# First cross attention: the rows of the context laid out by partition, 24 KB in one run instead of twelve runs of 2 KB

## The chip, the core and the metric

One core of one Trainium2 chip. The time is that of one execution on the device, in microseconds; of the kernel before there are three runs, and the number compared is their median.

## What is computed

A two-layer Perceiver block on x (8 batches of 64 rows of 512) and a context `ctx_1024` (8 batches of 1601 rows of 512), all float32. Every layer is a cross attention, an attention and an FFN, each added to x. The change lies in the very first of them:

```python
ex = jnp.einsum('bld,ed->ble', ix, W) + b          # ix = layernorm(x)
eother = jnp.einsum('bld,ed->ble', iother, W) + b  # iother = the context
scores = jnp.einsum('bld,bmd->blm', ex, eother)
attn = jax.nn.softmax(scores, axis=-1)
aligned = jnp.einsum('blm,bmd->bld', attn, iother)
```

The rest (a WKV recurrence, a product-key FFN, a 16-head cross attention on the same context, a sliding-window attention and a quantized linear layer) is as before.

## The kernel before, in words

The program is written by hand for each engine: every engine has its own list of instructions, and semaphores order them. All loads are issued by SyncE (SP), in the order in which its list has them, onto one DMA queue. Each waits only for the semaphore that tells that its buffer is free. A load raises its own semaphore by 16 when it has landed.

The first cross attention works on pairs of batches, p = 0 to 3 (a pair is 2 x 64 rows of x, so all 128 partitions). With g = W(Wx + b), computed on TensorE by the helper `product` (L416, matmuls at L420), the scores of a pair are g times the context, and the output is the softmax times the context. So the context is needed in two layouts:

- **Columns** (`load_columns`, L586 to 589, from `in_ctx_t`): the context transposed, the contraction over partitions. A pair has four pieces c = 0 to 3 of 4, 4, 2 and 3 tiles of 128 keys (`PIECE_TILE`, L63); each piece is two loads (one for each batch of the pair) into the slots of piece c. The host has already laid this array out by partition, so a partition's part of a piece is one run: 512 keys x 4 x 4 B = 8 KB for pieces 0 and 1, 4 KB for piece 2, 5 KB for piece 3. Piece c of pair p waits until the scores of piece c of pair p - 1 are done (`s1`, L602 to 604).
- **Rows** (`load_rows`, L580 to 584, from `in_ctx`): the context as it is, keys on the partitions, 12 full tiles of 128 rows in one load of 3072 KB (L583) and the last 65 rows in one of 130 KB (L584), for each of the two batches. Partition p of tile t is row 128 t + p, so a partition takes twelve runs of 2 KB, 256 KB apart. There are two sets of buffers (`cn`, L371); pair p >= 2 waits for the outputs of pair p - 2 (`pv1`, L606).

SP's order is: x, the two forms of W and the vectors (L575 to 578), columns (0, piece 0), (0, piece 1), rows(0); after the first layernorm columns (0, 2) and rows(1); after the g products (L598, L599) columns (0, 3); then for p = 1, 2, 3 the four pieces of columns(p), and for p = 2 and 3 rows(p) behind them (L601 to 607). Behind all that come the weights of the next layer (L609, L610), and after the last output those of the FFN (L613 to 617; `in_f` at L617 is read in runs of 4 KB with 16 KB from one partition's run to the next, `in_f` at L620 in runs of 2 KB).

TensorE goes through the pairs in the order `ORDER1` (L52 to 60): s(0), s(1), pt(0), o(0), s(2), pt(1), o(1), s(3), pt(2), o(2), pt(3), o(3). Here s is `scores1` (L957 to 971, matmuls at L968; piece c waits for its columns at L962), pt is `probabilities1` (transposes of the exponentials, L979), and o is `outputs1` (L982 to 994, 52 matmuls at L992, 13 tiles by two batches; it waits for the rows at L985). s(p) goes into the score banks of `SC` or `SB` by p's parity. Between s and pt, VectorE takes the maximum (`maximum1`, L1319) and ScalarE the exponential; after pt both copy the transposed probabilities out (L916, L918), and after o VectorE adds the output to X (L1337), which also frees the banks for s(p + 2) (L959, L960).

Of the kernel before, what the change touches and what calls it, by code (L numbers as in the profile page):

```python
# [12 lines left out]
P = 128  # L13
B, T, D = 8, 64, 512
NC = D // P
NT = B * T // P
M = 1601
MF = M // P
MR = M - MF * P
# [55 lines left out]
def piece_n(c, pad=0):  # L75

    k = piece_keys(c)
    return k.stop - k.start + pad * ((k.stop - k.start) % 2)
# [210 lines left out]
MID = 4  # L289


def build(nc, x, ctx_, W0, vecs, Wk, Wv, Wr, Wo, ctrl, f1, f2, Wq4, Wk4, Wv4,
          Wp4, bp4, Wq5, Wk5, Wv5, Wo5, wq, ws, bq, W0t, ctxt, tie, out):
    x = x.rearrange("b t d -> (b t) d").rearrange("(tt p) d -> p tt d", p=P)
    out = out.rearrange("b t d -> (b t) d").rearrange("(tt p) d -> p tt d", p=P)
# [4 lines left out]
    with ExitStack() as es:  # L300
# [8 lines left out]
        def sem(name):  # L309
            if name not in sems:  # L310
                sems[name] = es.enter_context(nc.semaphore(name))
            return sems[name]
# [75 lines left out]
        def inc(ins, name, by=1):  # L388
            return ins.then_inc(sem(name), by)
# [183 lines left out]
        def _(sp):  # L573
# [6 lines left out]
            def load_rows(p):  # L580
                for w in range(2):
                    dst, b, name = cn[p % 2][w], 2 * p + w, f"cn{p % 2}{w}_in"
                    inc(sp.dma_start(dst[:, 0:MF, :], ctx_[b, 0:MF * P, :].rearrange("(t p) d -> p t d", p=P)), name, 16)  # L583
                    inc(sp.dma_start(dst[0:MR, MF, :], ctx_[b, MF * P:M, :]), name, 16)  # L584

            def load_columns(p, c):  # L586
                n, at = NC * piece_n(c, 1), NC * piece_keys(c).start
# [3 lines left out]
            load_columns(0, 0)  # L591
            load_columns(0, 1)
            load_rows(0)
            for tt in range(NT):
                sp.wait_ge(*filled("ln0", tt))
            load_columns(0, 2)
            load_rows(1)
            sp.wait_ge(*filled("g", 3))  # L598
            sp.wait_ge(*filled("exb", 0))  # L599
            load_columns(0, 3)  # L600
            for p in range(1, NT):  # L601
                for c in range(KC):  # L602
                    sp.wait_ge(sem("s1"), KC * (p - 1) + c + 1)
                    load_columns(p, c)
                if p >= 2:
                    sp.wait_ge(sem("pv1"), p - 1)  # L606
                    load_rows(p)
# [1136 lines left out]
def laid_out(inputs):  # L1744


    import numpy as np

    ctx = inputs["ctx_1024"]
    padded = np.concatenate([ctx, np.zeros((B, M % 2, D), ctx.dtype)], axis=1)  # L1750
    pieces = [padded[:, PIECE_TILE[c] * P:][:, :piece_n(c, 1)] for c in range(KC)]

    ctx_t = np.concatenate([c.reshape(B, -1, NC, P).transpose(0, 3, 2, 1).reshape(B, P, -1) for c in pieces], axis=2)

    def by_head(w):

        return w.T.reshape(2, 4, 2, HD, D).transpose(0, 2, 1, 3, 4).reshape(D, D)

    laid = {
        "x": inputs["x"], "ctx": ctx, "W0": inputs["L0_xattn_W"],  # L1760
        "vectors": np.concatenate([inputs[n].reshape(-1, P).T for n in _VECTORS], axis=1),
        "Wk": inputs["L0_attn_Wk"].T, "Wv": inputs["L0_attn_Wv"].T, "Wr": inputs["L0_attn_Wr"].T,
        "Wo": inputs["L0_attn_Wo"].T,
        "controller": inputs["L0_ffn_controller"], "f1": inputs["L0_ffn_f1"], "f2": inputs["L0_ffn_f2"],
        "Wq4": inputs["L1_xattn_Wq"].T, "Wk4": inputs["L1_xattn_Wk"].T, "Wv4": inputs["L1_xattn_Wv"].T,
        "Wp4": inputs["L1_xattn_Wp"].T, "bp4": inputs["L1_xattn_bp"],
        "Wq5": inputs["L1_attn_Wq"].T, "Wk5": inputs["L1_attn_Wk"].T, "Wv5": inputs["L1_attn_Wv"].T,
        "Wo5": by_head(inputs["L1_attn_Wo"]),

        "wq": np.ascontiguousarray(inputs["L1_ffn_weight_q"].T).view(np.int32),  # L1770
        "ws": inputs["L1_ffn_weight_scale"], "bq": inputs["L1_ffn_bias"],
        "W0t": inputs["L0_xattn_W"].T, "ctx_t": ctx_t,

        "tie": np.repeat(np.linspace(0.0, 1e-6, NE, dtype=np.float32), ES)[:, None],
    }
    return {name: np.ascontiguousarray(a) for name, a in laid.items()}
# [16 lines left out]
```

## Time and profile before

| | us |
|---|---|
| median of 3 runs (lowest, highest) | 1229.19 (1227.73, 1231.67) |
| the profiled execution's own time | 1230.53 |
| its span | 1228.8 |
| lies outside the span (1230.53 - 1228.8) | 1.7 |

The profile and all its views are of that one execution. Its times count from the start of the span. TensorE is busy for 93% of the span, the 16 DMA engines for about a quarter of it, nearly all of that in the first sixth. A granted clock of 1.00 is TensorE's full speed of 2.4 GHz and 0.50 is 1.2 GHz. The DMA share of a stretch is summed over packets that overlap, so it can be a little over 1.

### The profile page before, as it was taken

The page shows a single profiled execution, that of the slowest core. Times are in us where ns is not written, and L with a number is a line of the kernel's source. Part 1 is how long each engine was busy: PE and PEld are TensorE (multiplying, and loading weights), DVE is VectorE, ACT ScalarE, POOL GpSimd, SP SyncE. Part 2 cuts the span into 40 slices and gives each one's busy share as a digit, 9 for nine tenths or more (in the row PEclk, how much of TensorE's full clock was granted, in tenths as well). Part 3 has the DMA queues.
Part 4 walks back from the last instruction along what each step waited for, and adds up shares of the span by engine and source line. Part 5 has one row for each costly group of instructions (what it writes and reads, how often), then busy time and mean ns, then how long its engine had stood idle before and what let it go on. Part 6 is the DMA issues. An engine that isn't in the chain of part 4 may idle for free.

```text
span 1228.8 us, 34222 instructions
## 1 busy us (share of the span) xinstructions
PE 1148.2 (93%) x15680; PEld 853.1 (69%) x15680; DVE 619.9 (50%) x978; ACT 433.2 (35%) x824; POOL 320.0 (26%) x362
## 2 busy tenths in 40 slices
PE   6879979878799999999999999999999999999996
PEld 3434434368488788788788888788878878866573
DVE  2011159564512545645555554554555554576667
ACT  1010053124233433433433433533443533343543
POOL 0000000014000233334233424243333243362612
PEclk9989989989799999999999999999999999999999
DMA  9999981253101101101100200111110110230000
GB/s 352 359 416 326 386 325 65 92 184 122 61 18 57 36 20 58 36 19 37 57 19 24 71 19 24 36 36 32 46 37 19 57 37 19 84 122 2 20 1 35
DMA packets 38880, 115.68 MB, mean 94 GB/s; under 512 B 2504, under 2 KB 3016, under 8 KB 34640
## 3 DMA queue, kind: packets, MB, share of 16 engines
q1 hardware_dynamic: 38736, 113.50, 25.9%
q8 instruction: 123, 2.02, 0.7%
q14 instruction: 21, 0.17, 0.0%
HBM read 112.44 MB, written 1.05 MB: 92 GB/s over the span
## 4 chain that ended last, share of the span: by engine, by line
PE 78%; ACT 5%; SPq 5%; DVE 4%; DMA 4%; issue 2%; POOL 1%; DVEq 0%; POOLq 0%; ACTq 0%
PE SB L429 45%; PE SC L1171 6%; PE SB L420 5%; SPq L584 4%; PE SB L1201 4%; DMA R<-in_ctx_t 2%; PE SB L992 2%; PE SB L1237 2%; ACT R L1685 2%; PE SC L1180 2%; DMA R<-in_ctx 2%; PE SC L1164 1%; PE SB L1060 1%; PE SC L968 1%; PE SB L1048 1%
## 5 line engine op out<-in xcount | busy, mean ns | idle before, releaser
L1685 ACT COPY R<-SB 64x512 f32<-64x512 f32 (+1 forms) x224 | 116.4, 520 | 201.5 <-PE SB L429 199.7
L429 PE MATMUL SB<-high,whigh 128*128 128x512 f32 (+2 forms) x512 | 180.0, 352 | 1.0 <-ACT Z L442 1.0
L1488 DVE TENSOR_REDUCE LN<-SC 128x64 f32<-128x768 f32 x128 | 116.6, 952 | 125.9 <-PE SC L1171 125.9
L429 PE MATMUL SB<-high,wlow 128*128 128x512 f32 (+2 forms) x512 | 178.7, 349 | 0.0
L429 PE MATMUL SB<-low,whigh 128*128 128x512 f32 (+2 forms) x512 | 177.2, 346 | 0.0
L429 PE MATMUL SB<-wlow,high 128*128 128x512 f32 (+1 forms) x416 | 167.8, 403 | 0.0
L429 PE MATMUL SB<-whigh,high 128*128 128x512 f32 (+1 forms) x416 | 166.1, 399 | 0.0
L429 PE MATMUL SB<-whigh,low 128*128 128x512 f32 (+1 forms) x416 | 165.7, 398 | 0.0
L727 POOL TENSOR_TENSOR added<-Z 128x768 f32<-128x768 f32 x32 | 58.7, 1836 | 281.7 <-ACT Z L1717 281.7
L727 POOL TENSOR_TENSOR added<-LN 128x768 f32<-128x768 f32 x32 | 58.6, 1830 | 264.9 <-ACT LN L1717 264.9
L429 PEld LDWEIGHTS SB<-high,whigh 128*128 128x128 f32 x512 | 96.6, 189 | 13.6 <-issue 1.4
L429 PEld LDWEIGHTS SB<-high,wlow 128*128 128x128 f32 x512 | 96.7, 189 | 11.6
L1712 ACT COPY LN<-SC 128x128 f32<-128x128 f32 x64 | 17.0, 266 | 248.3 <-PE SC L1180 247.8
L429 PEld LDWEIGHTS SB<-low,whigh 128*128 128x128 f32 x512 | 96.8, 189 | 9.6
L1463 DVE COPY R<-SB 128x512 f32<-128x512 f32 (+1 forms) x104 | 70.8, 686 | 51.7 <-PE SB L429 50.8
L429 PEld LDWEIGHTS SB<-wlow,high 128*128 128x128 f32 (+1 forms) x416 | 77.7, 187 | 19.1
L429 PEld LDWEIGHTS SB<-whigh,high 128*128 128x128 f32 (+1 forms) x416 | 77.6, 187 | 17.9
L429 PEld LDWEIGHTS SB<-whigh,low 128*128 128x128 f32 (+1 forms) x416 | 77.6, 187 | 17.7
L1503 DVE TENSOR_TENSOR Z<-SC,LN 128x768 f32<-128x768 f32 x64 | 58.3, 952 | 59.2 <-ACT LN L1712 59.0
L1503 DVE TENSOR_TENSOR LN<-SC,LN 128x768 f32<-128x768 f32 x64 | 58.3, 952 | 50.2 <-ACT LN L1712 50.2
L1171 PE MATMUL SC<-qb,R 32*64 32x64 f32 x6144 | 80.3, 231 | 0.0
L1469 DVE TENSOR_TENSOR low<-R,high 128x2048 fp32r<-128x2048 f32 (+2 forms) x32 | 58.1, 1815 | 43.4 <-ACT high L1674 43.4
(224 smaller groups left out, 1823.2 us busy)
## 6 DMA issues: line engine op xcount, KB each, us to landing
R<-in_ctx_t SPq DMA_DIRECT2D x32, 1024.0 KB, 8.2
R<-in_ctx SPq DMA_DIRECT2D x8, 3072.0 KB
R<-in_ctx_t SPq DMA_DIRECT2D x16, 644.0 KB, 6.8
R<-in_f SPq DMA_DIRECT2D x4, 2048.0 KB, 15.5
R<-in_f SPq DMA_DIRECT2D x1, 8192.0 KB, 25.7
R<-in_ctx_t SPq DMA_DIRECT2D x12, 512.0 KB, 3.6
R<-in_Wk SPq DMA_DIRECT2D x3, 1024.0 KB, 10.5
R<-in_Wv SPq DMA_DIRECT2D x3, 1024.0 KB, 8.9
```

Of the source, the lines that this page charges most:

```text
L420: last = pe.matmul(bk[:, :], lhs(k), rhs(k), start=k == 0, stop=k == NC - 1)
L429: last = pe.matmul(out_, lhs[a][:, k, :], rhs[b][:, k, :], start=n == 0, stop=n == 3 * NC - 1)
L584: inc(sp.dma_start(dst[0:MR, MF, :], ctx_[b, MF * P:M, :]), name, 16)
L727: inc(pool.tensor_tensor(added[:, :], p4_flat[w][0], p4_flat[w][1], ALU.add), "added4")
L992: last = pe.matmul(banks[w * T:(w + 1) * T, out1_at], pt1[0:n, t, w * T:(w + 1) * T], cn[u][w][0:n, t, :], start=t == 0, stop=t == KT_N - 1)
L1171: last = pe.matmul(sc_half[g][64 * j:64 * j + 64, r, a * T:(a + 1) * T], keys[u][rows, x, a * P + 64 * j:a * P + 64 * j + 64], qb[rows, x, ...
L1201: last = pe.matmul(BK[3][j * HD:(j + 1) * HD, pairs * T:(pairs + 1) * T], vals[side][0:m, t, h * HD:(h + 1) * HD], probabilities, start=t ...
L1463: inc(dve.tensor_copy(dst, src(BK[n])), f"read4_{n}")
L1469: inc(dve.tensor_tensor(low_r[c % 2][:, 0:n], low[c % 2][:, 0:n], high_r[c % 2][:, 0:n].bitcast(F32), ALU.subtract), "split")
L1488: inc(dve.tensor_reduce(tops[:, r * T:(r + 1) * T], sc_head[:, :, r, 0:6 * T].rearrange("p g (a q) -> p q g a", q=T), AX.XY, ALU.max), "ha ...
L1503: inc(dve.tensor_tensor(p4_half[x % 2][g], sc_half[g][:, :, 0:6 * T].rearrange("p r (a q) -> p r a q", q=T), top.unsqueeze(2).to_broadcast ...
L1685: last = act.copy(keys[nu][64 * half:64 * half + 64, pairs, first * P:first * P + full], src[:, :, 0:full])
```

## The change

The host hands over the first 1536 rows of each batch's context in another order, [batch, partition, tile, 512], so that the twelve rows that a partition takes lie side by side: 12 x 2 KB = 24 KB in one run, with 24 KB from one partition's run to the next. The last 65 rows become an array of their own, `ctx_end`. The kernel's two loads read from the new arrays into the same places of the same buffers, with the same semaphores. Nothing else changes, neither what is computed nor the order of any engine's instructions.

```diff
-def build(nc, x, ctx_, W0, vecs, Wk, Wv, Wr, Wo, ctrl, f1, f2, Wq4, Wk4, Wv4,
+def build(nc, x, ctx_, ctx_end, W0, vecs, Wk, Wv, Wr, Wo, ctrl, f1, f2, Wq4, Wk4, Wv4,
           Wp4, bp4, Wq5, Wk5, Wv5, Wo5, wq, ws, bq, W0t, ctxt, tie, out):
...
             def load_rows(p):
                 for w in range(2):
                     dst, b, name = cn[p % 2][w], 2 * p + w, f"cn{p % 2}{w}_in"
-                    inc(sp.dma_start(dst[:, 0:MF, :], ctx_[b, 0:MF * P, :].rearrange("(t p) d -> p t d", p=P)), name, 16)
-                    inc(sp.dma_start(dst[0:MR, MF, :], ctx_[b, MF * P:M, :]), name, 16)
+                    inc(sp.dma_start(dst[:, 0:MF, :], ctx_[b]), name, 16)
+                    inc(sp.dma_start(dst[0:MR, MF, :], ctx_end[b]), name, 16)
...
-        "x": inputs["x"], "ctx": ctx, "W0": inputs["L0_xattn_W"],
+        "x": inputs["x"], "ctx": ctx[:, :MF * P].reshape(B, MF, P, D).transpose(0, 2, 1, 3),
+        "ctx_end": ctx[:, MF * P:], "W0": inputs["L0_xattn_W"],
```

## Rows read from the trace of the kernel before

**Rows 1.** The page, parts 1 and 2: TensorE's busy time; DMA by slices.
```profile
PE 1148.2 (93%) x15680; PEld 853.1 (69%) x15680; DVE 619.9 (50%) x978; ACT 433.2 (35%) x824; POOL 320.0 (26%) x362
...
DMA  9999981253101101101100200111110110230000
GB/s 352 359 416 326 386 325 65 92 184 122 61 18 57 36 20 58 36 19 37 57 19 24 71 19 24 36 36 32 46 37 19 57 37 19 84 122 2 20 1 35
```

**Rows 2.** The chain that ended last, 43 to 155 us: start, length, what.
```profile
43.58 8.31 SPq L584
...
52.97 12.82 DMA R<-in_ctx_t
...
70.80 11.27 DMA R<-in_ctx_t
...
86.77 11.40 PE SC L992 x52
...
99.06 11.03 PE SC L968 x80
...
112.32 11.39 PE SB L992 x52
...
124.15 11.27 SPq L584
...
135.88 18.48 DMA R<-in_ctx
```

**Rows 3.** TensorE in order of time: start, length, instructions, [idle before <- releaser].
```profile
65.83 4.55 PE L968 MATMUL SC<-R,LT 128*64 128x256 f32 x32 [7.73 <-DMA R<-in_ctx_t]
...
82.11 2.41 PE L968 MATMUL SB<-R,LT 128*64 128x256 f32 x32 [0.94 <-DMA R<-in_ctx_t]
...
125.63 8.96 PE L968 MATMUL SB<-R,LT 128*64 128x512 f32 x33 [1.94 <-DMA R<-in_ctx_t]
...
138.60 1.64 PE L979 MATMUL SC<-ident,Z 128*128 128x128 f32 x13
...
154.45 11.38 PE L992 MATMUL SB<-R,Z 128*64 128x512 f32 x52 [0.58 <-DMA R<-in_ctx]
```

**Rows 4.** Stretches: from:to, length, granted clock, DMA share, GB/s.
```profile
12.00:20.00 8.00, 1.00 1.02 424
22.00:28.00 6.00, 1.00 1.05 387
...
60.00:62.00 2.00, 0.77 1.08 296
64.00:94.00 30.00, 0.88 1.01 417
96.00:100.00 4.00, 1.00 0.21 51
...
136.00:142.00 6.00, 1.00 1.05 387
172.00:180.00 8.00, 0.50 1.02 415
247.00:257.00 10.00, 0.66 1.05 386
```

**Rows 5.** DMA packets of the stretches 22 to 28, then 13 to 20.
```profile
DMA packets 1124, 2.32 MB, mean 387 GB/s; under 512 B 3, under 2 KB 3, under 8 KB 1120
...
DMA packets 407, 2.95 MB, mean 421 GB/s; under 512 B 47, under 2 KB 47, under 8 KB 47
```

**Rows 6.** SP's issues in order of time: start, length.
```profile
7.58 14.07 SPq L584 DMA_DIRECT2D R<-in_ctx  x1
...
51.99 6.47 SPq L589 DMA_DIRECT2D R<-in_ctx_t  x7
```

**Rows 7.** A stretch at the low clock: busy us (instructions) by engine, clock, DMA, GB/s.
```profile
126.00:129.00 3.00, 3.00 (x10) 1.10 (x8) 0.00 (x0) 0.00 (x0) 0.00 (x0) 0.50 0.99 406
```

**Rows 8.** The page, part 3: the queue that brings instructions.
```profile
q8 instruction: 123, 2.02, 0.7%
```

## The prediction

> **What bounds the kernel now.** I read the page first, then the chain of waits over the stretch that the change touches, then TensorE in order of time, and last the rate of DMA in single stretches. The page shows a kernel bound by TensorE (93% busy), but also a first sixth in which DMA is at 9 tenths and more; after that it is rarely above 3 [rows 1]. So the change can act only there. The chain says where inside that sixth it can. Up to 82 us it runs through DMA: the landing at 65.79 of piece 3 of columns(0), then that of columns(1) at 82.07 (70.80 + 11.27) [rows 2]. TensorE stood idle 7.73 us for the first [rows 3], and from there back to the start the queue shows no gap [rows 1]. From 82 us TensorE's own work is the chain, s, o, s, o, to 123.71; then come two waits for DMA again: 1.94 us before s(3) for columns(3), and 0.58 us before o(3), put down to rows(3) [rows 2, 3]. Behind 166 us nothing waits for the context's rows any more.
>
> **How fast the rows come now.** Two stretches that hold only row loads both show 387 GB/s [rows 4], in packets of 2 KB (1124 packets, 2.32 MB) [rows 5]. The 12 to 20 us stretch holds columns with runs of 8 KB: 424 GB/s [rows 4], and its 360 packets of 8 KB and up (407 less 47) carry nearly all of 2.95 MB, so a run is one packet [rows 5]. Two loads elsewhere say that the run's length makes the difference, not the array: runs of 4 KB at L617 go at 415, runs of 2 KB at L620 at 386 [rows 4]. The DMA share is about 1 in all of these, so the queue is full and the engines themselves set the rate.
>
> **What the change does, step by step.**
>
> 1. *The large row load (L583), eight of them.* Each moves 1536 x 2048 B = 3.146 MB. At 387 GB/s that is 8.13 us. The new run of 24 KB is longer than any in the rows, so I bound it. Lower bound of the gain: the rate of 4 KB runs, 415, gives 7.58 us, 0.55 saved. Upper bound: a packet's time on one of 16 engines is 2048 x 16 / 387 = 84.7 ns for 2 KB and 8192 x 16 / 424 = 309 ns for 8 KB, a fixed 9.9 ns plus 36.5 ns for each 1000 B; 24,576 B then take 908 ns, 433 GB/s, and the load 7.26 us, 0.87 saved. I take the nearest row, 8 KB at 424: 7.42 us, **0.71 us saved by each load**.
> 2. *The small one (L584), 65 rows.* Same runs, same shape, another array: nothing. The dip to 296 GB/s that goes with it (60 to 62 us) [rows 4] stays.
> 3. *SP's queue.* SP is held for 14.07 us at L584 behind the first large load, and 8.31 and 11.27 us later [rows 6, 2]; the seven column loads from 51.99 on take 6.47 us together [rows 6]. With a twelfth as many runs the hold should go. I cost this at nothing: the order on the queue is the same, and what SP can issue earlier stands behind work that keeps the queue full. Piece 3 of columns(0), issued at 51.99, would be issued as soon as its own wait (L599) is over, some us earlier, but the row loads ahead of it still fill the queue then. If the cover were gone, the price is still nothing, since the hold only gets shorter. The weights at L610 may be issued some us earlier and are needed only behind o(3) and a layernorm.
>
> Now the path. Ahead of the landing at 65.79 stand rows(0) and rows(1), four large loads: it comes 4 x 0.71 = 2.84 us earlier. The columns(1) behind it keep the queue full up to 82.07 (417 GB/s from 64 to 94 [rows 4]), so that landing moves by 2.84 too, and so does all of TensorE's own chain to 123.71, now 120.87. Rows(2) are issued by o(0)'s end, at a time when the queue has run empty (51 GB/s at 96 to 100) [rows 4], so they too start 2.84 earlier and then save 2 x 0.71 = 1.42 for the columns(3) behind them. Those land 4.26 earlier: piece 0 at 121.3 instead of 125.6. TensorE is ready at 120.87, so the wait before s(3) shrinks from 1.94 to about 0.5. Inside s(3) the pieces are paced by DMA: from 125.6, 2.1 MB for piece 1, 1.05 for piece 2 and 1.32 for piece 3 at 424 take 10.5 us, which is 136.1, and s(3) ends 2.4 us after (as piece 3 of s(1) does at 82.11 [rows 3]), at 138.6, where pt(2) starts [rows 3]. So the end of s(3) moves by **6 x 0.71 = 4.26 us**, to 134.3.
>
> The last two large loads, rows(3), land 8 x 0.71 = 5.7 earlier, at 148.7; o(3) would be ready for them at 154.45 - 4.26 = 150.2. The 0.58 us before o(3) is not won as well: pt is followed by as long a gap before o in the other pairs, in which VectorE and ScalarE copy the probabilities out. Hidden, gain zero. Late next is TensorE itself. Everything behind waits on o(3) or on loads issued behind it, and moves along. Sum: -4.26 us, against the profiled execution 1230.53 - 4.3 = 1226.3; that one was 1.3 above the median, so against the median 1229.19 - 4.3 = **1224.9**. About 0.3%, 3.7 us, is what a measurement of this kernel can tell from no change.
>
> On the run's length the Trainium skill speaks against this change: DMA: Bandwidth & Descriptors, Specifications, gives 512 B as the least transfer for line rate, by which 2 KB runs should lose nothing and the sum would be 0. The trace does not agree, 387 against 424.
>
> **The rivals.**
>
> *A, the forecast*, 0.63: 1224.9, by itself 1224.0 (0.87 a load, 5.2 us) to 1225.9 (0.55 a load, 3.3 us). For it: the rate goes with the run in four stretches. Against: no row has a 24 KB run.
>
> *B, the rate doesn't rise*, 0.13: the transfer is cut into 2 KB packets whatever lies beside them, or another limit than the run (the writes into the twelve rows' places, say) holds 387. Then all terms are 0: 1229.2. For it: nothing but that 24 KB isn't shown. Against: 8 KB runs go as one packet [rows 5].
>
> *C, TensorE gives a part back in s(3)*, 0.17. In the kernel before, an idle of 1.94 us ahead of s(3) was followed by a clock of 0.50 from 126 to 129 us [rows 3, 7]. In the new one piece 0 is worked off at full clock by 124.9 while piece 1 lands at 126.3: an idle of 1.4 us moves inside s(3). If the clock falls for as long behind that one, piece 1 takes 1.7 us more (32 matmuls of piece 3 took 4.55 us at 0.50 and 2.41 at full clock [rows 3]), ends at 131.5, and pieces 2 (1.8) and 3 (2.4) follow on without waiting, to 135.7. Gain 138.6 - 135.7 = 2.9 us: 1226.3, not to be told from no change.
>
> *D, long runs are slow*, 0.07, the one on the other side. The longest packets in the trace are those of the instruction queue: 123 packets with 2.02 MB took 0.7% of 16 engines' span, 0.007 x 16 x 1228.8 / 123 = 1.12 us for 16 KB, half the speed of the 8 KB packets [rows 8]. If that were due to their length, a 24 KB run takes 1.68 us, a large load (8 runs an engine) 13.4 us, 5.3 more than now, and six of them on the path cost 32 us: 1261. It decides from the point at which a 24 KB run takes longer than 12 x 84.7 ns = 1.02 us. Against it: those packets go to another place, in between others. The new spacing of 24 KB between partitions would be a second way to slower reads, but L617 reads at 415 with 16 KB [rows 4]. The Trainium skill has a rule of that kind (DMA: Bandwidth & Descriptors, Latency and other measured facts: a large power of two between the rows of an HBM array lowers the rate); its cases begin at 512 KiB, and no run here shows it.
>
> **How the numbers follow.** The likeliest is A, 1224.9. The range holds A and C with about 2 us for the spread of runs (the three shown lie 3.9 apart) below, 1221.7, and reaches above to B's 1229.2, which leaves D and the tails out. Faster by over 0.3%: A less its lower end, 0.60. Within: B, C and that end, 0.33. Slower: D, 0.07.
>
> **What would show it.** In the profile after: stretches inside the row loads at 424 or more with packets of over 8 KB, a twelfth as many of them; L584 held for under 1 us; TensorE's start after the long idle at 63.0 instead of 65.83; piece 3 of s(1) at 79.3; s(3) starting at 121.4 and pt(2) at 134.3, with the clock near 1.00 in between; o(3) at 150.2 with its rows landed over 1 us before; and from there on every stage shifted by the same 4.3 us. Row loads at 387 make it B; a pt(2) at 135.7 behind a clock of 0.50 makes it C; a first landing later than 65.8 makes it D. It would also be wrong if the shift were there at 150 us but gone by 300.

## The result, and the profile after

The changed kernel takes 1222.73 us (median of 13 runs, 1217.34 to 1226.33); the kernel before took 1229.19 in 13 runs of the same set. The ratio is 0.9945, with a 95% interval of 0.993 to 0.9961: 6.5 us or 0.5% faster, somewhere from 4.8 to 8.6 us. A second set gave 0.9954 (0.9935 to 0.9972). The forecast was 1224.9 in a range of 1221.7 to 1229.2, so it holds, with a gain that was set too small (4.3 us). The profiled execution took 1224.33 us with a span of 1222.6, 6.2 us under the span before.

The page after, parts 1 and 2, with the count of DMA packets:

```profile
PE 1148.8 (94%) x15680; PEld 851.6 (70%) x15680; DVE 620.4 (51%) x978; ACT 433.0 (35%) x824; POOL 320.1 (26%) x362
...
DMA  9999980434001101101100200111110110230000
DMA packets 27616, 115.68 MB, mean 95 GB/s; under 512 B 2504, under 2 KB 3016, under 8 KB 22352
```

Against [rows 1]: TensorE's work is the same (1148.8 and 1148.2 us), the bytes are the same, and packets fell from 38880 to 27616, by 11,264, which is 8 x (1536 - 128): each large row load is now one packet for each partition. So the gain is waiting that TensorE loses, and it arises in the first sixth: o(3) starts 6.7 us earlier. Of that, 4.8 us are left at the first matmul of the second cross attention (321.20 and 316.42 us) and 6.2 at the end of the span; the last section looks at the stage between.

The same stretch of packets as the first line of [rows 5], 22 to 28 us, now:

```profile
DMA packets 106, 2.61 MB, mean 434 GB/s; under 512 B 0, under 2 KB 0, under 8 KB 0
```

106 packets of 24 KB at 434 GB/s, where 1124 of 2 KB went at 387. In five other profiles with the same large loads, the same stretch shows 427 to 444, so 434 is good to about 2%. TensorE in order of time, against [rows 3] (start, length, instructions, [idle before <- releaser]):

```profile
61.53 3.32 PE L968 MATMUL SC<-R,LT 128*64 128x256 f32 x32 [2.43 <-DMA R<-in_ctx_t]
...
78.08 2.41 PE L968 MATMUL SB<-R,LT 128*64 128x256 f32 x32 [1.22 <-DMA R<-in_ctx_t]
...
120.57 7.59 PE L968 MATMUL SB<-R,LT 128*64 128x512 f32 x33 [0.91 <-DVE X L1337]
...
129.97 2.41 PE L968 MATMUL SB<-R,LT 128*64 128x256 f32 x32 [0.29 <-DMA R<-in_ctx_t]
132.32 1.64 PE L979 MATMUL SC<-ident,Z 128*128 128x128 f32 x13
...
147.73 11.38 PE L992 MATMUL SB<-R,Z 128*64 128x512 f32 x52
```

Piece 3 of s(0) starts 4.3 us earlier (65.83 to 61.53), piece 3 of s(1) 4.0 (82.11 to 78.08), s(3) 5.1, pt(2) 6.3 (138.60 to 132.32), o(3) 6.7 (154.45 to 147.73), and o(3) waits for no load any more: it starts 0.14 us behind the end of pt(3) (145.95 + 1.64), as against 0.58. Before s(3), TensorE waits 0.91 us for VectorE's addition to X instead of 1.94 for the columns.

The chain that ended last, 43 to 155 us, against [rows 2]:

```profile
48.59 12.89 DMA R<-in_ctx_t
...
65.25 12.78 DMA R<-in_ctx_t
...
106.44 23.49 DMA R<-in_ctx_t
```

Up to 78 us the chain still runs through the columns' landings, so the queue is still the bound there, and again from 106 to 130 us, up to the landing of the last piece of columns(3). SP's hold at L584, which stood in the old chain with 8.31 and 11.27 us, is gone from it. SP in order of time:

```profile
7.53 0.46 SPq L584 DMA_DIRECT2D R<-in_ctx_end  x1
...
18.21 4.63 SPq L584 DMA_DIRECT2D R<-in_ctx_end  x1
```

14.07 us became 0.46, and the longest hold left at L584 is 4.63. The holding as such isn't gone: seven column loads (L589) now take SP 11.24 us from 48.22 on, where the kernel before had 6.47 from 51.99 on.

### The profile page after: what moved, and what is told of

Its sections match the earlier page's. It is cut to its first block, busy times and chain, and to the rows that moved or that the text cites. A ratio compares the mean times of both kernels' runs of the same rounds, so it can differ in the third digit from the quotient of the medians.

```text
span 1222.6 us, 34222 instructions
## 1 busy us (share of the span) xinstructions
PE 1148.8 (94%) x15680; PEld 851.6 (70%) x15680; DVE 620.4 (51%) x978; ACT 433.0 (35%) x824; POOL 320.1 (26%) x362
## 2 busy tenths in 40 slices
DMA packets 27616, 115.68 MB, mean 95 GB/s; under 512 B 2504, under 2 KB 3016, under 8 KB 22352
## 4 chain that ended last, share of the span: by engine, by line
PE 82%; ACT 5%; DVE 5%; DMA 5%; issue 2%; POOL 1%; SPq 0%; DVEq 0%; POOLq 0%; ACTq 0%
PE SB L429 45%; PE SB L420 7%; PE SC L1171 6%; DMA R<-in_ctx_t 4%; PE SB L1201 4%; PE SC L992 2%; PE SB L1237 2%; ACT R L1685 2%; PE SC L1180 2%; PE SC L1164 1%; PE SB L1060 1%; PE SB L1048 1%; PE SC L968 1%; PE SB L1220 1%; PE SB L413 1%
## 5 line engine op out<-in xcount | busy, mean ns | idle before, releaser
L429 PE MATMUL SB<-high,whigh 128*128 128x512 f32 (+2 forms) x512 | 180.3, 352 | 1.0 <-ACT Z L442 1.0
L429 PE MATMUL SB<-high,wlow 128*128 128x512 f32 (+2 forms) x512 | 178.8, 349 | 0.0
L429 PE MATMUL SB<-low,whigh 128*128 128x512 f32 (+2 forms) x512 | 177.3, 346 | 0.0
L429 PE MATMUL SB<-wlow,high 128*128 128x512 f32 (+1 forms) x416 | 167.5, 403 | 0.0
L429 PE MATMUL SB<-whigh,high 128*128 128x512 f32 (+1 forms) x416 | 165.2, 397 | 0.0
L429 PE MATMUL SB<-whigh,low 128*128 128x512 f32 (+1 forms) x416 | 165.0, 397 | 0.0
L429 PEld LDWEIGHTS SB<-high,whigh 128*128 128x128 f32 x512 | 96.6, 189 | 13.6 <-issue 1.4
L429 PEld LDWEIGHTS SB<-high,wlow 128*128 128x128 f32 x512 | 96.7, 189 | 11.8
L429 PEld LDWEIGHTS SB<-low,whigh 128*128 128x128 f32 x512 | 96.8, 189 | 9.7
L429 PEld LDWEIGHTS SB<-wlow,high 128*128 128x128 f32 (+1 forms) x416 | 77.2, 186 | 19.0
L429 PEld LDWEIGHTS SB<-whigh,high 128*128 128x128 f32 (+1 forms) x416 | 77.1, 185 | 18.1
L429 PEld LDWEIGHTS SB<-whigh,low 128*128 128x128 f32 (+1 forms) x416 | 77.3, 186 | 17.5
```

The source lines that it names most:

```text
L429: last = pe.matmul(out_, lhs[a][:, k, :], rhs[b][:, k, :], start=n == 0, stop=n == 3 * NC - 1)
```

## The experiments

The theory: a packet costs some 10 ns beside its bytes, so the length of the run sets the rate; six of the eight large loads stand ahead of something that TensorE waits for. The rivals: the order of the addresses or SP's hold makes the gain; or it lies in other loads than I counted. Every ratio is to the kernel before in the same set. A single profile is one execution: of the kernels that load rows(0) and rows(1) as the kernel before did, piece 3 of s(0) starts at 65.83, 65.54, 64.96 and 64.93 in four profiles, so differences under 1 us between profiles say nothing. With these loads in 24 KB runs the spread is larger: 61.53, 62.13, 62.98 and, the outlier, 64.32.

### The new layout, cut into the old runs

```diff
-inc(sp.dma_start(dst[:, 0:MF, :], ctx_[b]), name, 16)
+inc(sp.dma_start(dst[:, 0:MF, :], ctx_[b], max_dma_last_dim=2048), name, 16)
```

> The new layout, with each load's runs cut into pieces of 2048 B again: the addresses are those of the changed kernel, the number of packets and SP's holds those of the kernel before. Run-length theory (a packet costs about 10 ns beside its bytes): row loads back at 387 GB/s, piece 3 of s(0) starts at 65.8 again, time 1229 (ratio 1.000, within 0.002). Rival, the order of the addresses makes the gain: row loads stay at 430 or more, piece 3 of s(0) starts near 61.5, time 1223 (ratio 0.995).

Measured: 1228.21 us, ratio 0.9997 (0.9981 to 1.0013). Packets of 22 to 28 us, then SP, then TensorE:

```profile
DMA packets 1129, 2.32 MB, mean 387 GB/s; under 512 B 2, under 2 KB 2, under 8 KB 1127
```
```profile
7.42 14.22 SPq L584 DMA_DIRECT2D R<-in_ctx_end  x1
```
```profile
65.54 4.55 PE L968 MATMUL SC<-R,LT 128*64 128x256 f32 x32 [6.34 <-DMA R<-in_ctx_t]
...
124.58 8.96 PE L968 MATMUL SB<-R,LT 128*64 128x512 f32 x33 [1.80 <-DMA R<-in_ctx_t]
...
153.40 11.38 PE L992 MATMUL SB<-R,Z 128*64 128x512 f32 x52 [0.57 <-DMA R<-in_ctx_end]
```

With the addresses of the changed kernel and the packets of the one before, everything of the one before is back: 387 GB/s, the hold of 14.22 us, all three waits, and the time. The order of the addresses in the array has no part in the gain. This run doesn't part the rate from SP's hold, since both come back; the next does in part (no run keeps SP's long hold with long packets).

### Runs of 8 KB

The same edit with `max_dma_last_dim=8192`.

> The new layout with runs cut into 8192 B. Run-length theory: row loads at 424 GB/s, 0.16 us slower for each large load than whole runs of 24 KB, so piece 3 of s(0) starts at about 62.1 and the time is within 1 us of the changed kernel's: 1223 to 1224 (ratio 0.995 to 0.996). Rival, only a run as long as the whole row of a partition helps (a load is then one packet for each partition): rate near 387 to 400, ratio over 0.998.

Measured: 1222.27 us, ratio 0.9961 (0.9941 to 0.9981).

```profile
DMA packets 311, 2.55 MB, mean 425 GB/s; under 512 B 0, under 2 KB 0, under 8 KB 0
```
```profile
62.63 3.83 PE L968 MATMUL SC<-R,LT 128*64 128x256 f32 x32 [3.92 <-DMA R<-in_ctx_t]
```

The rate is that of the columns' 8 KB runs. So the row loads have gone at 387, 425 and 434 GB/s with runs of 2, 8 and 24 KB. The fixed part worked out from the first two gave 433 for the third. SP's holds at L584 were up to 6.95 us here (before: 14.07); the queue stayed full behind them all the same (DMA share 1.00 or more in every stretch from 8 to 44 us). Most of the gain is reached at 8 KB. But its o(3) waits 0.70 us for the last small load of rows(3), which lands at 148.51, so at 8 KB rows(3) are not quite hidden.

### One pair at a time

Both arrays are handed over, and `load_rows` takes the new one for some pairs only:

```diff
+if p in (0, 1):
     inc(sp.dma_start(dst[:, 0:MF, :], ctx_[b]), name, 16)
+else:
+    inc(sp.dma_start(dst[:, 0:MF, :], ctx_old[b, 0:MF * P, :].rearrange("(t p) d -> p t d", p=P)), name, 16)
```

> New layout for rows(0) and rows(1) only, the old one for rows(2) and rows(3). Run-length theory with TensorE waiting for the queue only in s(0), s(1) and s(3): piece 3 of s(0) near 61.5 and of s(1) near 78.1 as in the changed kernel; s(3) is paced by DMA again and ends 4.0 us before the kernel before, not 6.3; a wait of about 0.4 us for rows(3) before o(3) comes back. Time 4.0 to 4.4 us below the kernel before: 1225 (ratio 0.9965). Rival, the gain lies in the late loads or in SP's hold: ratio over 0.998 here.

Measured, pairs 0 and 1: 1226.18 us, ratio 0.9977 (0.9961 to 0.9993).

```profile
64.32 3.92 PE L971 MATMUL SC<-R,LT 128*64 128x256 f32 x32 [6.64 <-DMA R<-in_ctx_t]
...
80.26 2.41 PE L971 MATMUL SB<-R,LT 128*64 128x256 f32 x32 [0.59 <-DMA R<-in_ctx_t]
...
123.64 3.65 PE L971 MATMUL SB<-R,LT 128*64 128x512 f32 x16 [1.75 <-DMA R<-in_ctx_t]
...
136.60 1.64 PE L982 MATMUL SC<-ident,Z 128*128 128x128 f32 x13
...
152.65 11.38 PE L995 MATMUL SB<-R,Z 128*64 128x512 f32 x52 [0.78 <-DMA R<-in_ctx_end]
```

Its own gain is clear, and the waits at s(3) and o(3) come back as expected, but piece 3 of s(0) starts at 64.32, not near 61.5, and pt(2) is 2.0 us ahead of the kernel before, not 4.0. It is a miss that I can't settle: with the same large loads ahead of that piece, three other profiles have 61.53, 62.13 and 62.98. The rate around the small loads is lower here (297 GB/s from 56 to 60 us, where the changed kernel has 329). This kernel holds one array more, so its arrays may lie elsewhere in HBM; that wasn't tried. What this run shows for rows(0) and rows(1) is thus the whole time, not the place in the trace.

> New layout for rows(2) only. Run-length theory: nothing moves up to 98 us; the columns(3) behind rows(2) land 1.7 us earlier, so the 1.94 us before s(3) shrink to about 0.9 (then TensorE waits for the addition to X instead), and s(3) ends 1.7 us earlier. Time 1.7 to 2.1 us below the kernel before: 1227.3 (ratio 0.9984). Rival, only what lies before 82 us counts: ratio 1.000.

Measured, pair 2: 1227.58 us, ratio 0.9998 (0.9981 to 1.0015). The time can't tell 1.7 us from none; the profile can.

```profile
124.44 3.65 PE L971 MATMUL SB<-R,LT 128*64 128x512 f32 x16 [0.91 <-DVE X L1340]
...
136.52 1.64 PE L982 MATMUL SC<-ident,Z 128*128 128x128 f32 x13
```

From pt(0) to pt(2) it takes 136.52 - 84.28 = 52.2 us; the kernel before took 138.60 - 84.45 = 54.1, pairs 0 and 1 alone 54.0 (136.60 - 82.61), the changed kernel 51.9 (132.32 - 80.42). So rows(2) give about 1.9 us in this stretch, in place of my 1.42, and the wait before s(3) is already VectorE's. In all four profiles with 2 KB runs for rows(2) the stretch takes 53.9 to 54.2 us, in the four with 24 KB runs and the same order 51.9 to 52.5.

> New layout for rows(3) only. My count says that its two large loads are hidden: TensorE waits 0.4 us for them at most, before o(3). Time 0.0 to 0.4 us below the kernel before: 1229 (ratio 0.9997 to 1.000, within what can be told). Rival, rows(3) are on the path (the weights behind them come late, or o(3) is gated by them): 1.5 us or more, ratio 0.9988 or less, and a first matmul of the next layer that moves relative to o(3).

Measured, pair 3: 1228.95 us, ratio 1.0 (0.9987 to 1.0014).

```profile
150.79 1.64 PE L982 MATMUL SB<-ident,Z 128*128 128x128 f32 x13
152.57 11.38 PE L995 MATMUL SB<-R,Z 128*64 128x512 f32 x52
```

o(3) starts 0.14 us behind pt(3), with no wait for a load: rows(3) are worth the 0.4 us of that wait, and no more. So rows(2) are on the path and rows(3) off it but for that wait, as counted; for rows(0) and rows(1) only the time speaks, with the miss above. The three times alone don't prove the sum: their gains (by the ratios 2.8, 0.2 and 0.0 us) add up to 3.0, give or take about 3.

### The changed kernel again

> The changed kernel once more, as the yardstick of this set on the same chip: ratio 0.9945 as before (within 0.002). Its profile also tells how far the starts of piece 3 of s(0) (61.5 in the first profile) and of o(3) (147.7) repeat: if single profiles of one kernel lie 1 us or more apart there, differences of that size between my other profiles mean nothing.

Measured: 1222.4 us, ratio 0.9954 (0.9935 to 0.9972).

```profile
62.13 4.09 PE L968 MATMUL SC<-R,LT 128*64 128x256 f32 x32 [3.29 <-DMA R<-in_ctx_t]
...
148.26 11.38 PE L992 MATMUL SB<-R,Z 128*64 128x512 f32 x52
```

The two profiles lie 0.6 us apart at piece 3 of s(0) and 0.5 at o(3). The gain is the same as in the first set.

### The small loads

The rate is not even in the row loads. Stretches of the changed kernel (from:to, length, granted clock, DMA share, GB/s):

```profile
28.00:32.00 4.00, 1.00 1.01 353
...
56.00:60.00 4.00, 1.00 0.95 329
```

The 65 rows (L584) fall into these. First they were padded to 80, which 16 divides (`dst[0:80, MF, :]`, `ctx_end` with 15 rows of zeros for each batch):

> The changed kernel with the last 65 rows padded to 80, so that the small load has 5 rows for each of 16 engines (15 rows of zeros more, which nothing reads). In the changed kernel the stretch from the first row load to piece 3 of columns(0) is longer than its large loads by about 0.8 us for each small one, at rates down to 250 GB/s. Theory, the 65 rows go by on fewer engines and in long gaps: a small load costs 0.4 us, piece 3 of s(0) starts 1.4 us earlier (60.1), everything up to o(3) by as much: time 1221.3 (ratio 0.9933 to 0.9940). Rival, the dip is the small load's start and end whatever its shape: no change, or 0.1 us slower, for the padding: ratio 0.9945.

Measured: 1223.85 us, ratio 0.9957 (0.9937 to 0.9978); piece 3 of s(0) starts at 62.98, not at the 60.1 of the theory, and the dips are where they were:

```profile
28.00:32.00 4.00, 1.00 1.02 354
...
56.00:60.00 4.00, 1.00 0.95 322
```

So it isn't the number 65. Then the last tile went into the large load, filled up to 128 rows with zeros:

```diff
-inc(sp.dma_start(dst[:, 0:MF, :], ctx_[b]), name, 16)
-inc(sp.dma_start(dst[0:MR, MF, :], ctx_end[b]), name, 16)
+inc(sp.dma_start(dst[:, :, :], ctx_[b]), name, 16)
```

> All 1601 rows of a batch in one load: 13 rows for each partition in one run of 26 KB, the last tile filled up with zeros (63 rows that nothing reads); no small loads any more. In the changed kernel the rate falls to 320 to 350 GB/s for some 4 us around each small load. Theory, the small load is the cause: the dips go, a pair of loads is 7.9 us instead of about 8.3 to 8.7, piece 3 of s(0) starts 1.5 to 3 us earlier than in the changed kernel's profile of the same set, and 1 to 2 us of it reach the end: ratio 0.993. Rival, the dip comes wherever one load follows another of long runs: it stays at the same places, and nothing is gained: ratio 0.9945.

Measured: 1220.53 us (6 runs), ratio 0.994 (0.9924 to 0.9957).

```profile
28.00:32.00 4.00, 1.00 1.02 439
...
56.00:60.00 4.00, 1.00 1.02 419
```
```profile
60.73 2.41 PE L967 MATMUL SC<-R,LT 128*64 128x256 f32 x32 [1.64 <-DMA R<-in_ctx_t]
...
145.74 11.38 PE L991 MATMUL SB<-R,Z 128*64 128x512 f32 x52
```

The dips are gone, though each batch moves 126 KB more. Piece 3 of s(0) starts 0.8 to 1.4 us earlier than in the two profiles of the changed kernel, o(3) 2.0 to 2.5. So the dip belongs to the small load, not to the change from one load to the next. Its packets being shorter than those around it can't be the whole reason: the kernel before has the dip too (296 GB/s from 60 to 62 us), where the row loads next to it are in 2 KB packets themselves. Why it costs stays open. In the whole time its ratio can't be told from the changed kernel's.

### Another order

Rows(1) are needed only by o(1), at 108 us, but half of their bytes could be moved behind columns(1):

```diff
 load_columns(0, 2)
-load_rows(1)
+load_rows(1, (0,))
...
                     load_columns(p, c)
+                if p == 1:
+                    load_rows(1, (1,))
```

> The changed kernel with the second batch of rows(1), not needed before o(1) at 108 us, issued behind columns(1) instead of ahead of piece 3 of columns(0). If the landings at 61.5 and 78.1 are late only for the bytes ahead of them in the queue: no wait before piece 3 of s(0), s(1) ends near 71 instead of 80.5; then the queue has the same bytes to bring before s(3) and o(3) and takes some back: s(3) waits about 2 us again and ends near 126 instead of 134.3 of the forecast, o(3) starts near 141.5 instead of 147.7. Time 1216.5 (ratio 0.9895). Rival, the queue is short of bandwidth throughout, so order can't win: waits move from s(1) to s(2) and s(3), and the time stays at 1222 to 1223 (ratio 0.9945).

Measured: 1224.07 us, ratio 0.9955 (0.9938 to 0.9971). Stretches of the queue, then TensorE:

```profile
48.00:50.00 2.00, 0.50 0.72 173
...
52.00:54.00 2.00, 1.00 0.23 95
```
```profile
118.02 9.77 PE L970 MATMUL SB<-R,LT 128*64 128x512 f32 x33 [3.52 <-DMA R<-in_ctx_t]
...
146.85 11.38 PE L994 MATMUL SB<-R,Z 128*64 128x512 f32 x52
```

The wait before piece 3 of s(0) is gone and o(0) starts 5 us earlier, as expected, but s(3) then waits 3.52 us, and of the 6 us expected at o(3) 1 is left. The queue ran partly empty twice near 50 us and was full from 56 to 124, so I read the wait as the bytes that it had not moved before; the split below tests that. Behind that wait the granted clock was 0.50 from 117 to 123 us, and 33 matmuls of s(3) took 9.77 us where those of the run with merged loads (26 KB runs), at full clock and without a wait, took 7.30: up to 2.5 us of the loss are the clock's. My working had let rows(2) start as soon as they were issued, at 89 us, with columns(2) still in the queue.

> Both edits, the padded small loads and the new order. If the small loads' cost is real and s(3) is then bound by the queue, 6 of them at 0.35 us come on top: 1214.5 (ratio 0.988). If the padding is worth nothing, as order alone.

Measured: 1224.48 us, ratio 0.9958 (0.9942 to 0.9975): as the order alone. s(3) waits 4.79 us here; the padding is worth nothing again.

So the batch was cut in two, six tiles behind piece 3 of columns(0), to fill the gap near 53 us, and the rest behind columns(1), to fill the one near 93:

```diff
+def load_part(lo, hi):
+    inc(sp.dma_start(cn[1][1][:, lo:hi, :], ctx_[3][:, lo:hi, :]), "cn11_in", 16)
...
 load_columns(0, 3)
+load_part(0, 6)
...
+if p == 1:
+    load_part(6, MF)
```

> The changed kernel with the second batch of rows(1) in two halves of six tiles: one behind piece 3 of columns(0), one behind columns(1). In the run with the order changed, the queue ran empty near 48 and near 53 us and was full from 55 to 124, while the changed kernel's queue was empty near 92 to 96. Theory, every microsecond in which the queue is empty before s(3) is paid at s(3): with both gaps filled s(3) starts 3 us earlier than with the whole batch moved (115 instead of 118.0), o(3) at about 144, time 3 us below the changed kernel's (ratio 0.992). Rival, the wait moves to TensorE's own chain or to the clock (s(3) at 0.50 for longer, as the order run had): ratio 0.9945 to 0.9955.

Measured: 1217.46 us (6 runs, 1216.22 to 1224.04), ratio 0.9931 (0.9908 to 0.9955).

```profile
116.77 3.65 PE L976 MATMUL SB<-R,LT 128*64 128x512 f32 x16 [0.91 <-DVE X L1345]
...
144.84 11.38 PE L1000 MATMUL SB<-R,Z 128*64 128x512 f32 x52
```

The queue from 92 to 94 us, in the changed kernel and then here:

```profile
92.00:94.00 2.00, 1.00 0.05 21
```
```profile
92.00:94.00 2.00, 1.00 1.04 430
```

The queue moves 430 GB/s, where the changed kernel's stood nearly still; no wait for columns at the start of s(3); o(3) 2.9 to 3.4 us earlier than in the changed kernel. That is the expected size at o(3).

> Both: loads of 26 KB runs, and the second batch of rows(1) in two parts (6 and 7 tiles). If the small loads cost what the theory says and the queue binds s(3), the gains add: ratio 0.990. If neither holds, as the changed kernel: 0.9945.

Measured: 1220.15 us (6 runs), ratio 0.9942 (0.9925 to 0.9958). Its o(3) is the earliest of all,

```profile
143.76 11.38 PE L997 MATMUL SB<-R,Z 128*64 128x512 f32 x52
```

4.0 to 4.5 us ahead of the changed kernel. The gains add only in part, even up to there: alone, the two edits give 2.0 to 2.5 and 2.9 to 3.4, and this kernel starts s(3) no earlier than the split alone (116.67 and 116.77), behind VectorE's addition to X. The forecast of 0.990 was missed. The last section shows where the rest goes in the profiled execution. The split version has the lowest median of all kernels run here, yet its interval overlaps the changed kernel's of the same set (0.9935 to 0.9972), so that it beats it is shown at o(3), not for the whole.

## Why the prediction was right, and by how much it was off

- **What bounds.** Right: the gain lies in the first sixth, and nearly all of it came through the landings of the columns behind the rows, not through the rows themselves.
- **Step 1, the large load.** The mechanism was right and the term too small. I took the nearest row, 424 GB/s, and 0.71 us a load; it was 434 GB/s, so 7.25 us instead of 8.13, 0.88 a load. The upper bound from a fixed part and a part by bytes (433) came out. Six loads are 5.3 us, not 4.26. With the 427 to 444 of the other profiles a load saves 0.76 to 1.04 us.
- **Step 2, the small load.** Its dip stayed, as said. That it could be taken away for 2 us I had not seen.
- **Step 3, SP.** The hold at L584 went (14.07 to 0.46, though one of 4.63 was left where I had said under 1) and I see nothing gained by it: the queue was full before and after. That is argued from the full queue; no run changes the hold alone.
- **The path.** Forecast, then measured in the first and the second profile: piece 3 of s(0) 63.0, 61.53, 62.13; piece 3 of s(1) 79.3, 78.08, 78.01; pt(2) 134.3, 132.32, 132.84; o(3) 150.2, 147.73, 148.26. The profile of the kernel before was itself a late one (65.83 against 64.93 to 65.54 in three others with the same early loads), which makes the gain at o(3) look up to 1 us larger than six loads of 0.88 and the wait at o(3) explain. Nor did every later stage shift by the same amount, as I had written: 6.7 us at o(3), 4.8 at the second cross attention, 6.2 at the end. The shift was not lost, though.
- **The wait before s(3).** I had it shrink to 0.5. It is 0.91, and VectorE's: I left out that s(3) also waits for the addition to X (L960), as s(2) did. It costs nothing, since s(3)'s end is paced by its last piece, which lands late (piece 3 still waits 0.29 us for it; it is in the chain after).
- **The wait before o(3).** This step failed: I wrote that the 0.58 us "is not won as well", since the other pairs have as long a gap. In the other pairs VectorE does the maximum first and copies then; in pair 3 it has no maximum, and the gap without a wait is 0.14. So 0.44 us were the rows' after all, and the run with pair 3 alone shows just that. It also means that the rows were less well hidden than I had them (over 1 us of room): with runs of 8 KB there was a wait left.
- **Rival B** fell with the 434 GB/s; the Trainium skill's figure behind it (DMA: Bandwidth & Descriptors, Specifications: at 512 B a transfer is at line rate) doesn't fit this kernel, in which 2 KB runs lose 11% against 24 KB. **Rival C** didn't come: the idle before piece 1 of s(3) was 0.3 us (0.61 in the second profile), not 1.4, and the clock stayed at 1.00. **Rival D** fell: long runs were the fastest.

Sum by the corrected terms: 6 x 0.88 + 0.44 = 5.7 us, inside the 4.8 to 8.6 that were measured. The interval is wide, so it can't confirm the size of a single term; the rates and the runs with one pair do that for step 1 and for pairs 2 and 3.

## What to carry to other kernels

In this kernel, while the DMA queue was full, bytes, bytes per run and short loads in between set when things landed: fit a packet's time as a fixed part plus a part by bytes from two stretches of the profile, and use the fit, not the nearest rate, for a longer run. Then count the loads that stand ahead of a wait, not all that get faster. To reorder a full queue moved a wait here; it gained only where it filled the queue's empty stretches. And a gap before an instruction is a load's fault only by what exceeds the same gap without that load, in the same place.

## What the runs showed of the hardware

**A stage behind the change takes one of two times.** From o(3) to the first matmul of the second cross attention (L429), none of these edits touches anything, and yet it took 168.7 and 168.5 us in the two profiles of the changed kernel (316.42 - 147.73, 316.75 - 148.26) and 163.4 in that with runs of 8 KB (312.03 - 148.60).

Stretches of the changed kernel, then of that with runs of 8 KB (the third column is the granted clock):

```profile
230.00:236.00 6.00, 0.79 0.70 237
236.00:242.00 6.00, 0.64 1.04 392
242.00:248.00 6.00, 0.64 1.05 386
248.00:254.00 6.00, 0.79 1.02 375
```
```profile
230.00:236.00 6.00, 1.00 0.60 216
236.00:242.00 6.00, 1.00 0.99 377
242.00:248.00 6.00, 0.72 1.05 387
248.00:254.00 6.00, 1.00 1.05 385
```

Between 230 and 254 us TensorE works in short pieces with waits between them, and its clock is at the low of its two levels (1.2 instead of 2.4 GHz) for more than half of the time in one execution and for a small part in the other. The same eight matmuls (L1026), in the changed kernel and in that with runs of 8 KB:

```profile
234.93 6.29 PE L1026 MATMUL SB<-LT,CW 128*64 128x512 f32 x8 [0.98 <-ACT LT L829]
```
```profile
235.10 3.62 PE L1026 MATMUL SB<-LT,CW 128*64 128x512 f32 x8 [0.98 <-ACT LT L829]
```

From their start to the first matmul of L1048 it is 22.8 us in one and 20.0 in the other (257.72 - 234.93, 255.10 - 235.10), so over half of the difference of 5 us arises here. In the 14 profiles the stage took 163.3 to 164.1 us five times, 168.0 to 168.9 eight times, and 166.8 in that of the kernel before. The split version's profile had 163.3 and that with both edits 168.8: of the 1.1 us that the second was ahead at o(3), nothing could be left. The times go with it: the five profiled executions with the short stage are 1.2 to 4.3 us faster than the median of their kernel, the eight with the long one from 0.2 faster to 3.1 slower. I take it that such swings make a large part of the 7 to 9 us between the fastest and the slowest run of one kernel. What decides between the two wasn't found, and whether a kernel can be made to fall on the short side wasn't tried.

**An idle of nearly 2 us can cost the clock, and need not.** Before s(3), TensorE was idle for 1.94 and 1.80 us in the kernel before and in that cut to 2 KB, and the clock was at 0.50 for about 3 us behind it; with 1.75 and 1.67 us (pairs 0 and 1, pair 3) it stayed up. But it also stayed up behind 1.90 us ahead of s(1) (both edits) and 1.86 ahead of its piece 3 (the other order), so the length of the idle alone doesn't tell.
